# Attention score matmuls in two halves of the array's rows, four query stacks, and a quantization step split between ScalarE and GpSimd

## The chip, the cores and the metric

The kernel runs on one core of one Trainium2 chip. The metric is the device time in microseconds, the median of three runs; lower is better. TensorE's clock has two levels, 1.2 and 2.4 GHz, and the profile shows the granted share as PEclk (1.00 is 2.4 GHz).

## What is computed

The input x has shape (4, 512, 512), and everything is in float32.

```python
xn = layernorm(x)
q = (xn @ wq) as 32 heads of 16;  k = xn @ wk;  v = xn @ wv   # one k and one v for all heads
scores = q k^T / sqrt(16), causal;  probs = softmax(scores)
s = (probs @ v) @ wo
def linear8bit(x, W, b):            # columns of x with absmax > 3 go unquantized
    y = quant_rows(x_inliers) @ quant_rows(W).T + x_outliers @ W.T + b
    # quant_rows: scale = absmax/127 of the row, round(a/scale) * scale
h = linear8bit(xn, W1, b1)          # W1 is 2048 x 512
g = silu(linear8bit(h, W2, b2))     # W2 is 512 x 2048
out = x + s * g
```

## The kernel before, in words

Accuracy near float32 comes from splitting each operand into a high part in fp32r (the type that TensorE streams in one pass) and a low part, which is what the high part leaves over. A product is the sum of high x high, high x low and low x high.

There are three stages, each a block in which every engine has its own hand-written queue, joined by semaphores, with a barrier of all engines between them.

1. Preparation: layernorm, transposes, q, k and v (`a_order`, lines 163 to 174). The queries stay in `big_h` and `big_l` with features on partitions. The keys are copied several times down the partitions into `km` and `ks`: six groups of 16 rows (line 182), of which a mask in `cols` keeps the three that belong to head parity p (lines 415 to 421), so that there are two versions, p = 0 and p = 1. GpSimd builds the masks and the two step patterns `later_q` and `later_k` (lines 230 to 288), which make later keys lose inside the diagonal block of the first pass.
2. Attention, in 16 units `u` of 8 heads, one unit for each batch and 128 features. For a unit, 12 transfers (`stack_queries`, line 151) copy queries into one of three stacks: 96 rows with two heads each (high, low, high), 4 rows for the row maxima and 28 of the step pattern. The first pass (`max_piece`, lines 972 to 993) computes scores with queries on partitions, and VectorE reduces each of 24 PSUM pieces of 256, 384 or 512 columns to row maxima (line 914). These are transposed (line 1052), copied by ScalarE (line 852), and put into the stack by one transfer (line 730), so that the second pass (`scores`, line 995) gives scores with the maximum subtracted and keys on partitions. ScalarE exponentiates 22 pieces of 384 or 512 columns (line 835), GpSimd masks the diagonal blocks (line 817), and TensorE multiplies by the values in four column groups of 32 (`pv`, line 1009). VectorE transposes and inverts sums, GpSimd divides, and the unit's rows go back to `big_h` and `big_l`. `project` (line 1033) multiplies the attended rows by `wo`. Beside this runs, for one tile of 128 rows in each unit, the quantization of xn (`quantize_x`, line 698): GpSimd masks the outlier columns, VectorE takes the absmax, the scale and the reciprocal, then in one instruction multiplies xn by it and adds the magic number (line 715), GpSimd takes the magic number off (line 790), ScalarE scales back (line 845).
3. The two large products of the feed-forward part (lines 1783 to 1785 and 1806 to 1808), which the change leaves as they are but for one wait.

The order of the attention stage is one counter `g` of steps, 24 a unit (`CH`). In each step every engine does its share in program order: TensorE first one first-pass piece, then one piece of scores of a unit whose steps run `CH + LAG` = 35 later, then what tables such as `PV_AT`, `NORM_AT` and `XSCALE_AT` (lines 607 to 624) place in that step. PSUM has three banks for the first pass (`MAXB`), three for scores (`STB`), one for probs x values (`PVB`) and one for all else. A first-pass piece n waits for the reduction of piece n - 3 (line 980), a scores piece for the exponential of piece n - 3 (line 1003):

```python
if n >= NMAX:
    pe.wait_ge(s_red, n - NMAX + 1)
...
if n >= NST:
    pe.wait_ge(s_exp, n - NST + 1)
```

Outside the steady part stand the first 35 steps, in which only the first pass runs, and the drain after the last first-pass piece: the scores of the last units, 12 tile transposes for the next stage (line 1078), and projections.

## Time and profile before

| | |
|---|---|
| median of 3 runs | 802.34 us (799.99 to 802.61) |
| profiled execution, its time | 802.84 us |
| its span | 801.1 us |
| TensorE matmul busy | 764.9 us (95%) |
| VectorE busy | 638.7 us (80%) |
| ScalarE busy | 402.7 us (50%) |
| GpSimd busy | 257.6 us (32%) |

The profile is one execution. Busy times are the union of an engine's instructions, from start to end. Instructions of one engine overlap at their ends, so the work of a queue is better read from the distance between the starts of two instructions that follow each other. Matmul ends are modelled. A bracket behind a row gives the idle time before it and what ended that.

### The profile page before, as it was taken

Reading aid. Unit: us, or ns where it says so; the run is one execution under the profiler, and the core shown is the slowest. Engines: PE = TensorE matmul, PEld = TensorE weight load, DVE = VectorE, ACT = ScalarE, POOL = GpSimd, SP = SyncE. Lnnn points to the kernel's source line nnn. Section 1 sums busy time; section 2 is a strip of 40 time slices with the busy share of each in tenths; the row PEclk is TensorE's granted clock in tenths of the full one; section 3 lists DMA queues with packets and bytes.
Section 4 is the critical chain, followed back from the end, with each engine's and each line's share of the span. In section 5 each row is a group of like instructions: output and inputs, shape, how many; then the busy total and the mean of one; then the engine's idle time right before and its main releaser. Section 6 shows DMA issues by size and latency. Waiting matters only on the chain. (4 is left out here: it accounts for less than half of the span.)

```text
span 801.1 us, 12089 instructions
## 1 busy us (share of the span) xinstructions
PE 764.9 (95%) x4253; PEld 579.5 (72%) x4253; DVE 638.7 (80%) x1094; ACT 402.7 (50%) x683; POOL 257.6 (32%) x335
## 2 busy tenths in 40 slices
PE   4999999999999999999999999999997999999995
PEld 3877665556676666775578888788886788888884
DVE  7988989999999899995537476666658998599957
ACT  3454166767677676777634554544553333122212
POOL 7313135555555555554621110110100000036504
PEclk9999589999999999999999999999999999999998
DMA  7421303333322223334554444222013778536982
GB/s 258 153 106 53 86 11 91 82 80 92 90 81 83 82 81 95 89 113 123 161 192 159 143 158 144 81 78 79 27 47 97 251 220 259 164 106 219 334 287 105
DMA packets 58348, 103.37 MB, mean 129 GB/s; under 512 B 8480, under 2 KB 16688, under 8 KB 56752
## 3 DMA queue, kind: packets, MB, share of 16 engines
q1 hardware_dynamic: 58288, 102.60, 40.3%
q8 instruction: 34, 0.56, 0.3%
q14 instruction: 26, 0.21, 0.1%
HBM read 52.76 MB, written 36.70 MB: 112 GB/s over the span
## 5 line engine op out<-in xcount | busy, mean ns | idle before, releaser
L914 DVE TENSOR_REDUCE rowmax<-ps 128x2 f32<-128x512 f32 (+3 forms) x384 | 210.9, 591 | 20.7 <-PE ps L991 18.8
L835 ACT ACTIVATE probs<-ps 128x512 f32<-128x512 f32 (+1 forms) x352 | 175.2, 557 | 72.4 <-PE ps L1004 70.7
L991 PE MATMUL ps<-km,stack 128*128 128x256 f32 (+3 forms) x512 | 151.0, 350 | 2.0 <-PEq L187 1.9
L1004 PE MATMUL ps<-stack,ks 128*128 128x512 f32 (+1 forms) x352 | 133.1, 388 | 2.6 <-ACT probs L835 2.6
L991 PEld LDWEIGHTS ps<-km,stack 128*128 128x128 f32 (+1 forms) x512 | 96.0, 201 | 42.2 <-DVE rowmax L914 22.5
L817 POOL TENSOR_SCALAR_AFFINE_SELECT probs<-probs 128x512 f32<-128x512 f32 x128 | 81.0, 641 | 79.1 <-ACT probs L835 77.6
L1806 PE MATMUL ps<-big_h 128*128 128x512 f32 x256 | 100.4, 392 | 2.4 <-issue 2.0
L1808 PE MATMUL ps<-big_h,big_l 128*128 128x512 f32 x256 | 100.3, 392 | 0.0
L1807 PE MATMUL ps<-big_l,big_h 128*128 128x512 f32 x256 | 100.2, 391 | 0.0
L1017 PE MATMUL ps<-probs,vones 128*32 128x512 f32 (+3 forms) x1024 | 82.2, 439 | 0.2 <-POOL probs L817 0.2
L1004 PEld LDWEIGHTS ps<-stack,ks 128*128 128x128 f32 x352 | 67.5, 192 | 11.9 <-ACT probs L835 6.3
L1806 PEld LDWEIGHTS ps<-big_h 128*128 128x128 f32 x256 | 48.3, 189 | 12.8 <-issue 3.0
L1017 PEld LDWEIGHTS ps<-probs,vones 128*32 128x32 f32 x1024 | 26.7, 109 | 41.3 <-issue 28.2
L1808 PEld LDWEIGHTS ps<-big_h,big_l 128*128 128x128 f32 x256 | 48.3, 189 | 10.2
L1807 PEld LDWEIGHTS ps<-big_l,big_h 128*128 128x128 f32 x256 | 48.3, 189 | 10.0
L1783 PE MATMUL ps<-big_h,w_high_first 128*128 128x512 f32 x128 | 51.9, 406 | 1.6 <-PEq L689 1.6
L1438 ACT ACTIVATE h_on<-ps,b_col,w_scale 128x512 f32<-128x512 f32 x36 | 28.0, 779 | 48.8 <-PE ps L1785 48.8
L1783 PE MATMUL ps<-big_h,w_high_second 128*128 128x512 f32 x128 | 51.9, 406 | 0.6 <-DVE w_low_second L1505 0.6
L1477 ACT CAST big_h<-habs 128x1024 fp32r<-128x1024 f32 x31 | 32.4, 1045 | 39.0 <-DVE habs L1586 23.3
L1784 PE MATMUL ps<-big_l,w_high_second 128*128 128x512 f32 x128 | 50.5, 395 | 0.0
L1785 PE MATMUL ps<-big_h,w_low_second 128*128 128x512 f32 x128 | 50.5, 395 | 0.0
L1784 PE MATMUL ps<-big_l,w_high_first 128*128 128x512 f32 x128 | 50.5, 395 | 0.0
(227 smaller groups left out, 1384.3 us busy)
## 6 DMA issues: line engine op xcount, KB each, us to landing
stack<-big_h SPq DMA_DIRECT2D x128, 64.0 KB, 2.0
h_scratch<-hs SPq DMA_DIRECT2D x7, 1024.0 KB, 4.5
hload<-h_scratch SPq DMA_DIRECT2D x14, 512.0 KB, 5.4
xn_scratch<-xa SPq DMA_DIRECT2D x4, 1024.0 KB, 4.4
stack<-big_l SPq DMA_DIRECT2D x64, 64.0 KB, 2.0
xi<-xn_scratch SPq DMA_DIRECT2D x16, 256.0 KB, 2.8
xe_scratch<-xm SPq DMA_DIRECT2D x16, 256.0 KB, 2.3
w2n<-in_L_ffn_W_dram SPq DMA_DIRECT2D x4, 1024.0 KB, 6.7
```

What stands on the lines that cost most here:

```text
L817: nc.gpsimd.affine_select(out=d, in_=d, compare_op=ALU.is_ge, fill=0.0, base=0, pattern=[[0, NPAIR], [1, P]], channel_multiplier=-1).then_ ...
L835: nc.scalar.activation(probs[p][:, o:o + nh * w], ps[:, STB[n % NST], 0:nh * w], ACT.Exp).then_inc(s_exp, 1)
L914: nc.vector.tensor_reduce(dst, src, AX_X, ALU.max).then_inc(s_red, 1)
L991: last = nc.tensor.matmul(dst, stack[u % 3][rows, hp, P * qt:P * (qt + 1)], km[rows, u // KT, p0:p0 + npar, keys], start=True, stop=True)
L1004: ins = nc.tensor.matmul(ps[:, STB[n % NST], 0:nh * w].rearrange("p (h q) -> p h q", h=nh), ks[:, u // KT, p, P * kt:P * (kt + 1)], stack[ ...
L1017: ins = nc.tensor.matmul(ps[32 * j:32 * j + 32, PVB, P * kt:T], vones[:, u // KT, kt, :], probs[p][:, o:o + w], start=(kt == 0), stop=(kt ...
L1783: nc.tensor.matmul(dst, w1h[f % 2][:, k, :], big_h[:, k, t], start=(k == 0), stop=False)
L1784: nc.tensor.matmul(dst, w1h[f % 2][:, k, :], big_l[:, k, t], start=False, stop=False)
L1785: last = nc.tensor.matmul(dst, w1l[f % 2][:, k, :], big_h[:, k, t], start=False, stop=(k == KT - 1))
L1806: nc.tensor.matmul(ps[:, i, :], hqh[m % RB][:, t], w2h[m % RB], start=(kk == 0), stop=False)
L1807: nc.tensor.matmul(ps[:, i, :], hqh[m % RB][:, t], w2l[m % RB], start=False, stop=False)
L1808: return nc.tensor.matmul(ps[:, i, :], hql[m % RB][:, t], w2h[m % RB], start=False, stop=(kk == FT - 1))
```

## The change

The two head groups of a unit now lie in partitions 0 to 63 and 64 to 127: in each half 48 rows of one head's query and key parts, 2 rows for the maxima and 14 of the step pattern (two finer patterns, 10 steps of 2^12 and a factor of 32). One version of `km` and `ks` serves both. Every score matmul becomes two, one in each half of the array's rows with a PSUM bank of its own, issued one behind the other. Pieces are packed to full banks: 20 reductions and 20 exponentials a unit, all of 512 columns, in place of 24 and 22. The columns of `wq` and rows of `wo` are reordered to fit, `wo` by eight transfers; a unit's queries come by 6 transfers of 128 KB instead of 12 of 64 KB, the maxima by two transfers instead of one. There are four stacks. A unit has 20 steps. In `quantize_x` the multiply-and-add of VectorE (line 715) goes: ScalarE multiplies by the scale, GpSimd adds the magic number and then takes it off. The last combination of the row maxima becomes a reduction of three rows (128x24 to 128x8).

```diff
-        km = sa("km", [P, B, 2, T], F32R)
-        ks = sa("ks", [P, B, 2, T], F32R)
+        km = sa("km", [P, B, T], F32R)
+        ks = sa("ks", [P, B, T], F32R)
+        NSTK = 4
+        HALF_ROWS, KEPT = P // 2, 3 * HD
...
-            for hp in range(NPAIR):
-                src = slice(2 * HD * hp, 2 * HD * (hp + 1))
+            for a in range(2):
+                src = slice(HALF_ROWS * a, HALF_ROWS * (a + 1))
                 for n, part in enumerate((big_h, big_l, big_h)):
+                    lo = HALF_ROWS * a + HD * n
+                    sp.dma_start(stack[u % NSTK][lo:lo + HD, :, :].bitcast(F32),
+                                 part[src, f, tok].bitcast(F32)).then_inc(s_sq[u % NSTK], 16)
...
-                        for p in range(2):
-                            step(nc.vector.tensor_scalar(km[:, g, p, :], kvh, cols[:, p:p + 1], None,
-                                                         ALU.mult))
...
+                        step(nc.vector.tensor_scalar(ks[:, g, :], kvh, cols[:, 0:1], None, ALU.mult))
+                        ins = nc.vector.scalar_tensor_tensor(out=ks[:, g, :], in0=kvl, scalar=cols[:, 1:2],
+                                                             in1=ks[:, g, :].bitcast(F32),
+                                                             op0=ALU.mult, op1=ALU.add)
...
-        CH = 24
+        CH, NB = 20, 10
+        def pieces_of(c):
+            v, m = divmod(c // 2, 5)
+            hp = 2 * v + m // 2
+            if m == 4:
+                return [(2 * v + h, 1, own, 2 * P * h + P * own) for h in range(2) for own in (False, True)]
+            if m % 2:
+                return [(hp, 2, False, 0), (hp, 2, True, 2 * P), (hp, 0, True, 3 * P)]
+            return [(hp, 3, False, 0), (hp, 3, True, 3 * P)]
+        def scores_of(i):
+            return [[(0, 0, 1, 0)], [(0, 1, 1, 0)], [(1, 0, 1, 0), (3, 0, 1, 3 * P)],
+                    [(1, 1, 1, 0), (3, 1, 1, 3 * P)], [(2, 0, 2, 0)]][i]
...
-        GROUPS = [(0, 1), (2, 3)]
+        GROUPS = [(0, 1, 3), (2,)]
...
-        LAG = 11
+        LAG = 10
-        PV_AT = {11: (0, 0), 16: (0, 1), 22: (1, 0), 27: (1, 1)}
-        NORM_AT = {19: 0, 27: 1, 30: 2, 33: 3}
-        SHARE_AT, HIGH_AT, LOW_AT = 30, 34, 33
-        XLOAD_AT, XMASK_AT, XSCALE_AT, XROUND_AT, XBACK_AT, XSTORE_AT = -1, 15, 21, 25, 26, 30
+        PV_AT = {10: (0, 0), 14: (0, 1), 18: (1, 0), 22: (1, 1)}
+        NORM_AT = {16: 0, 24: 1, 26: 2, 29: 3}
+        SHARE_AT, HIGH_AT, LOW_AT = 25, 29, 28
+        XLOAD_AT, XMASK_AT, XSCALE_AT, XROUND_AT, XBACK_AT, XSTORE_AT = -1, 12, 16, 22, 24, 28
...
-        EVENLY = (3, 7, 12, 16)
+        EVENLY = (3, 7, 11, 13)
...
-                if part == 3:
-                    dve.wait_ge(s_xst, 3 * i + 3)
-                    nc.vector.scalar_tensor_tensor(out=xm[:, :], in0=xi[:, :], scalar=xs[:, 0:1],
-                                                   in1=magic_row[:, :], op0=ALU.mult,
-                                                   op1=ALU.add).then_inc(s_xt, 1)
...
                     u = unit_at(g, XROUND_AT)
                     if u >= 0:
                         pool.wait_ge(s_xt, u + 1)
+                        nc.gpsimd.tensor_tensor(xm[:, :], xm[:, :], magic_row[:, :],
+                                                ALU.add).then_inc(s_xg, 1)
+                        pool.wait_ge(s_xg, u + 1)
                         nc.gpsimd.tensor_tensor(xm[:, :], xm[:, :], magic_row[:, :],
                                                 ALU.subtract).then_inc(s_xr, 1)
...
+                    u = unit_at(g, XSCALE_AT + 4)
+                    if u >= 0:
+                        act.wait_ge(s_xst, 3 * u + 3)
+                        nc.scalar.activation(xm[:, :], xi[:, :], ACT.Copy, scale=xs[:, 0:1]).then_inc(s_xt, 1)
...
+                def max_pair(u, c):
                     n = CH * u + c
...
+                    if n + 1 >= NMAX:
+                        pe.wait_ge(s_red, n + 2 - NMAX)
+                    pieces = pieces_of(c)
+                    for hp, qt, own, at in pieces:
                         keys = slice(P * qt, P * qt + P) if own else slice(0, P * qt)
+                        for a in range(2):
+                            rows = slice(HALF_ROWS * a, HALF_ROWS * a + (HALF_ROWS if own else KEPT))
+                            dst = ps[:, MAXB[(n + a) % NMAX], at:at + keys.stop - keys.start]
+                            ins = nc.tensor.matmul(dst, stack[u % NSTK][rows, hp, P * qt:P * (qt + 1)],
+                                                   km[rows, u // KT, keys], start=True, stop=True)
+                            if (hp, qt, own, at) == pieces[-1]:
+                                ins.then_inc(s_max, 1)
+
+                def score_pair(u, s):
+                    p, i = divmod(s // 2, NB // 2)
                     n = 2 * NB * u + s
                     if s == 0:
+                        pe.wait_ge(s_sm[u % NSTK], 32 * (u // NSTK + 1))
+                    if n + 1 >= NST:
+                        pe.wait_ge(s_exp, n + 2 - NST)
+                    parts = scores_of(i)
+                    for kt, h, nh, at in parts:
                         w = T - P * kt
+                        for a in range(2):
+                            rows = slice(HALF_ROWS * a, HALF_ROWS * (a + 1))
+                            dst = ps[:, STB[(n + a) % NST], at:at + nh * w].rearrange("p (h q) -> p h q", h=nh)
+                            ins = nc.tensor.matmul(dst, ks[rows, u // KT, P * kt:P * (kt + 1)],
+                                                   stack[u % NSTK][rows, 2 * p + h:2 * p + h + nh, P * kt:T],
+                                                   start=True, stop=True)
+                            if kt == parts[-1][0]:
+                                ins.then_inc(s_st, 1)
...
-                        max_piece(*divmod(g, CH))
+                    if g < CH * U and g % 2 == 0:
+                        max_pair(*divmod(g, CH))
...
+                    if u >= 0 and s_ % 2 == 0:
+                        score_pair(u, s_)
```

## Rows read from the trace of the kernel before

**Rows 1.** The page's slices of the span: the rows of TensorE and its clock.

```profile
PE   4999999999999999999999999999997999999995
...
PEclk9999589999999999999999999999999999999998
```

**Rows 2.** Busy time of one stretch: length, then each engine's busy time, PEclk, DMA share, GB/s.

```profile
240.00:260.00 20.00, 20.00 (x145) 13.78 (x147) 18.45 (x40) 14.41 (x30) 11.29 (x15) 1.00 0.29 83
```

**Rows 3.** Timeline of all engines in one unit (start, us): GpSimd's subtraction, twice.

```profile
245.22 1.29 POOL L790 TENSOR_TENSOR xm<-xm,magic_row 128x512 f32<-128x512 f32 x1 [2.77 <-DVE xm L715]
...
263.51 1.29 POOL L790 TENSOR_TENSOR xm<-xm,magic_row 128x512 f32<-128x512 f32 x1 [2.77 <-DVE xm L715]
```

**Rows 4.** The same timeline: matmuls of the two passes and of the projection.

```profile
247.33 0.39 PE L1042 MATMUL ps<-woh,big_h 128*128 128x512 f32 x1
...
247.55 0.40 PE L1043 MATMUL ps<-wol,big_h 128*128 128x512 f32 x1
...
248.20 0.34 PE L1004 MATMUL ps<-stack,ks 128*128 128x384 f32 x1
...
248.37 0.28 PE L991 MATMUL ps<-km,stack 128*128 128x256 f32 x1
...
248.49 0.34 PE L1004 MATMUL ps<-stack,ks 128*128 128x384 f32 x1
```

**Rows 5.** The same timeline: probs x values in four column groups, and what follows it.

```profile
245.67 0.86 PE L1017 MATMUL ps<-probs,vones 128*32 128x256 f32 x16
...
246.45 0.50 PE L991 MATMUL ps<-km,stack 128*128 128x256 f32 x2
...
251.28 1.71 PE L1017 MATMUL ps<-probs,vones 128*32 128x512 f32 x16
...
252.92 0.45 PE L991 MATMUL ps<-km,stack 96*128 96x384 f32 x1
...
253.20 0.40 PE L1004 MATMUL ps<-stack,ks 128*128 128x512 f32 x1
```

**Rows 6.** Timeline of VectorE in the same unit: a reduction of 512 columns and its follower.

```profile
260.45 0.68 DVE L914 TENSOR_REDUCE rowmax<-ps 128x4 f32<-128x512 f32 x1
261.05 0.14 DVE L708 TENSOR_SCALAR xs<-xs 128x1 f32<-128x1 f32 x1
```

**Rows 7.** Groups by line and form in the attention stage (busy us, mean ns).

```profile
L914 DVE TENSOR_REDUCE rowmax<-ps 128x2 f32<-128x512 f32 x128 | 81.8, 680 | 0.9 <-PE ps L991 0.6
...
L914 DVE TENSOR_REDUCE rowmax<-ps 128x1 f32<-128x384 f32 x128 | 68.2, 550 | 18.1 <-PE ps L991 17.2
...
L1017 PE MATMUL ps<-probs,vones 128*32 128x512 f32 x256 | 34.1, 605 | 0.0
...
L715 DVE SCALAR_TENSOR_TENSOR xm<-xi,xs,magic_row 128x512 f32<-128x512 f32 x16 | 11.9, 745 | 0.1
```

**Rows 8.** Timeline of ScalarE in the drain: an exponential and its follower.

```profile
385.30 0.63 ACT L835 ACTIVATE probs<-ps 128x512 f32<-128x512 f32 x1
385.79 0.64 ACT L840 CAST big_h<-tb 128x512 fp32r<-128x512 f32 x1
```

**Rows 9.** The same timeline: the way of the row maxima into the stack.

```profile
257.36 0.56 ACT L852 CAST w_low_first<-ps 16x512 fp32r<-16x512 f32 x1
...
257.95 0.69 SPq L730 DMA_DIRECT2D stack<-w_low_first  x1
```

**Rows 10.** DMA issues (the page's last part): KB each, median us to landing.

```profile
stack<-big_h SPq DMA_DIRECT2D x128, 64.0 KB, 2.0
```

**Rows 11.** Timelines of TensorE and VectorE where the attention stage begins.

```profile
81.53 14.68 PE L991 MATMUL ps<-km,stack 128*128 128x256 f32 x38 [1.90 <-PEq L187]
...
100.79 0.80 PE L1004 MATMUL ps<-stack,ks 128*128 128x512 f32 x1
```

**Rows 12.** Timeline of TensorE: first tile transposes in the drain, first matmul of stage 3.

```profile
363.91 0.63 PE L1078 MATMUL ps<-ident,tail_rows 128*128 128x128 f32 x4
...
408.99 0.47 PE L1783 MATMUL ps<-big_h,w_high_first 128*128 128x512 f32 x1 [1.62 <-PEq L689]
```

245 lines of the change are left out of this document (110 added, 135 removed).

## The prediction, made before the changed kernel ran

> **What bounds the kernel now.** I first read the slices of the span [rows 1]: TensorE is busy nearly throughout, and its clock is at the upper level except in one stretch near the start of attention. Then the busy time by stretch [rows 2]: from 240 to 260 us TensorE is busy for all 20 us and VectorE for 18.45. Both are close, so the bound has to be told by adding up queues. The unit's length comes from one instruction that each unit has once: it starts at 245.22 and at 263.51 us, 18.29 us apart [rows 3].
>
> TensorE's queue in a unit, by distances between starts [rows 4]: a matmul of 512 columns takes 0.23 us, one of 384 takes 0.18 (248.20 to 248.37), one of 256 takes 0.12. The first pass is, for each of four head pairs, one of 256, four of 256 (two pieces of two matmuls), one of 512 and two of 384: 5 x 0.12 + 0.23 + 2 x 0.18 = 1.19, so 4.8 us. The scores, for each of two parities, are seven of 512 and four of 384: 2.33, so 4.7 us. Probs x values takes 1.64 us for its first group (251.28 to 252.92) and 0.78 for its second (245.67 to 246.45) [rows 5]; twice each is 4.8, and with about 0.1 of wait on each side of the four groups (the next matmul begins 0.28 us after the one at 252.92, though 384 columns take 0.18) 5.6 us. The projection is 12 x 0.23 = 2.8 and the transposes of the maxima 0.6. The sum is 18.5 us, against 18.29 measured: TensorE's queue sets the unit.
>
> VectorE's queue: a reduction of 512 columns takes 0.60 us from start to start [rows 6], though its own duration is 0.68 [rows 7]; 0.08 overlaps. 384 columns take 0.55 less 0.08, 0.47 [rows 7], so 256 take 0.34. Four times (0.34 + 3 x 0.60 + 2 x 0.47) is 12.3 us; the three transposes 1.9, reciprocals 0.4, the quantization 0.73 and 0.66 for line 715 (0.745 less 0.08 [rows 7]), the maxima's small steps 0.5: 16.5 us. That is only 1.8 us below TensorE, and it caps the gain.
>
> **TensorE after the change.** The score matmuls hold the same 10,240 columns in each pass, but in pairs, one per half of the rows. Whether halves overlap is not shown by the trace of before, since every matmul there takes all rows. The nearest row is probs x values: in 128x32 form, the 256 matmuls of 512 columns last 605 ns each and yet add up to only 34.1 us of busy time [rows 7], 0.13 us each, so the four column groups run together. I take it that two row halves do the same; bounds are fully together and fully one behind the other.
>
> Together, a pair costs what one costs. A pair with 128 columns has no row; half of the 0.12 of 256 columns is its lower bound, 0.06, and the whole 0.19 that a weight load takes its upper. I take 0.11, nearest to the 0.12 at which a matmul and the load under it repeat. The first pass has, for each two heads of a half, two windows of (384, 128), two of (256, 128, 128) and one of four times 128: 2 x 0.29 + 2 x 0.34 + 0.44 = 1.70, so 3.4 us a unit. The scores have for each parity three of 512 and two of (384, 128): 1.27, so 2.5 us. Both together: 5.9 in place of 9.5, 3.6 us less.
>
> Against this stands a switch between forms. After the column-grouped matmuls the first full one starts late and its follower 0.1 later again [rows 5]: counted as 0.3 us for a round trip: about 0.1 at the way in, 0.1 before the matmul at 252.92 and 0.1 before its follower. Now the projection (four places a unit) and the maxima's transposes also stand as full-row work between half-row pairs: 5 more round trips. Bounds are 0 and 0.4 us each; I take 0.3, the measured kind, so 1.5 us. The sum is 5.9 + 5.6 + 2.8 + 0.6 + 1.5 = 16.4 us.
>
> The row [rows 5] shows that a form change costs TensorE about 0.3 us. The Trainium skill, page "TensorEngine Tiling (Array Packing)", section "Key Properties", says that a change of tiling mode drains the engine; that speaks against this change. By the rule all five new places pay, and the sum is the 16.4 above; were it wrong for row halves, it would be 14.9.
>
> **VectorE after the change.** 20 x 0.60 = 12.0 in place of 12.3; line 715 gone, -0.66; the three-row reduction against the old maximum, within 0.05 either way (24 inputs; 0 to 0.1 us). So 12.0 + 1.9 + 0.4 + 0.7 + 0.6 = 15.6 us.
>
> **How the queues meet.** Before, TensorE waited for the reduction three pieces back; now a pair waits for the one two before its second bank, so it may start when the first reduction of the pair ahead is done, and has only the second, 0.60 us, to deliver. From the wait to data it needs about 0.1 for the weights, the starts of the parts (0.18 to 0.33) and the last one's time of 0.2 to 0.25, so 0.55 to 0.75 us, where 0.60 is covered. That is 0.05 us on most pairs and 0.15 on the (4 x 128) ones, 0.4 us a unit when nothing else hides it. Then TensorE's two heavy windows: after steps 10 and 18 it does probs x values for key blocks 0, 1 and 3 at once. The first group of before has 7 column blocks in 1.64 us, 0.1 of it switch, so 0.22 a block; 8 blocks are 1.7 us, with the switch 2.0, with the pairs 2.5 and 2.7 us, while VectorE has 1.65 (the maxima's casts) and 1.3 us of work. A lead of 0.6 us is all that VectorE's queue can have; 0.3 and 0.8 us are lost. 15.6 + 0.4 + 1.1 = 17.1 us a unit.
>
> **ScalarE and GpSimd.** ScalarE: 0.49 us a start-to-start exponential of 512 columns [rows 8], 384 about 0.1 less (estimated from its fewer columns); 14 x 0.49 + 8 x 0.39 = 10.0 before, 20 x 0.49 = 9.8 after, and the new multiply. That has no row on ScalarE with this form; the scaling back at line 845 is 0.63 from start to start (bounds 0.49 to 0.63, I take 0.63). With 2.1 us of other work it is 12.5 of 17.1 us, covered; the waits of ScalarE for TensorE are what shrinks. GpSimd gets one more pass of 1.29 us [rows 3], 10.4 to 11.7 us a unit. It sits at step 22, ahead of the mask at step 3 of the next unit and ScalarE's scaling back at step 24; the mask is needed at step 10. If it is late, TensorE's probs x values waits, and all first-pass pairs behind it; seven steps of 0.85 us against about 4 us of GpSimd work cover it. At no cost.
>
> **Transfers.** The queries move the same 768 KB in half the issues and one unit earlier: nothing. The maxima: copy at 257.36, issue at 257.95, 0.69 us [rows 9]; the second issue adds 0.69. Before, some 4 us pass until the first scores; now from step 4 to step 10 there are 5.1 us at 0.85 a step, and copy, two issues and 2 us of landing [rows 10] are 3.9. Covered, with 1 us to spare; behind this wait stands all of TensorE.
>
> **Outside the steady part.** Preparation: VectorE has two more small low parts ahead of the first transposed rows, +0.3 us; the key steps saved and GpSimd's changed constants lie beside TensorE's work; wo's eight issues come while SyncE has nothing due. The first steps: 35 steps lasted from 81.53 to some 101.6 us [rows 11], 20.1 us, at the lower clock [rows 1]. Now 30 steps, 15 pairs of 1.2 us; at the lower level columns take twice as long, so about 0.25 us a pair is not covered: 15 x 1.45 = 21.8, +1.7 us. The drain lasts from 363.9 to 409.0 us [rows 12]; its 30 steps of scores in place of 35 spare TensorE 3 us, and its transposes between them add up to 12 round trips of which part is paid already: -1.5 us (-3 to +2).
>
> **The sum.** From the start of the scores (101.6) to the drain (363.9) the old kernel passes 349 steps, 0.752 us each, so 18.05 us for 24. That is 14.5 units: 14.5 x (18.05 - 17.1) = 13.8 us less. With +0.3, +1.7 and -1.5, the change is -13.3 us on the profiled execution's 802.84, so 789.5; that execution lies 0.5 above the median of 802.34, so the forecast is **789 us**.
>
> **Rivals.** (B) Row halves change place without a drain, and the lead is enough: VectorE sets the unit at 15.6 + 0.6 = 16.2. For it: between halves and full rows the columns' grouping stays the same. Against it: the form change that is shown does cost. 14.5 x 1.85 = 26.8 less, 776 us. (C) Halves don't overlap: the pairs cost 11.9 instead of 5.9 us, TensorE 22.4 us a unit, +4.3 x 14.5 = +62, about 864 us. Against it stand the overlapping column groups. It decides from the point at which a pair costs 1.3 times one matmul (5.9 x 1.3 = +1.8 us). (D) Half-row pairs overlap but their weight loads don't hide: 128 columns cost 0.19 and a round trip 0.4. There are 20 slots of 128 columns a unit, +1.6, and +0.5 for the switches: TensorE has 18.5 us, and with what the heavy windows lose 18.7: +0.65 x 14.5 = +9, 811 us. It needs both near their upper bounds, and is slower from 18.1 a unit on. (E) TensorE's clock stays at the lower level, which it had while only the first pass ran [rows 1], since it has idle time again: the queue of 16.4 us would be some 30, over 950 us. Against it: it rose once scores ran beside the first pass, and at the lower level TensorE would have no idle time.
>
> The Trainium skill, page "TensorE: Matmul & The Clock Gate", section "The mechanism" of its part on packing, says that loads and matmuls of different row groups overlap. By it C is wrong and A or B holds; no run here shows it yet.
>
> **How the numbers follow.** Chances: forecast (A) 0.52, B 0.18, C 0.10, D 0.17, E 0.03. A, B and D, with D's less complete forms, lie between 772 and 810. A difference under 0.3% (2.4 us) is no more than a measurement of this kernel can tell. A and B are faster; a third of D is within it or just faster. Faster 0.74, same 0.05, slower 0.21.
>
> **What would show it.** Two score matmuls a few ns apart, and a pair no longer than one (A, B, D); 17.1 us between two subtractions of line 790; VectorE busy over 90% with waits for the first pass after steps 10 and 18; a start about 0.3 us late after each projection; ScalarE's waits shorter; the lower clock still there in the first steps. The prediction is wrong if a pair takes two matmuls' time, if GpSimd's masks or the maxima's transfer hold TensorE, or if clock levels change within the steady part.

## The result, and the profile of the changed kernel

The changed kernel takes 809.89 us in the median of 4 runs (808.69 to 813.15), the kernel before 802.05 (799.99 to 802.61, 4 runs). The ratio is 1.0109, with a 95% interval of 1.0073 to 1.0145. The forecast was 789 us, range 772 to 810. The change made the kernel slower by 1.1% and not faster by 1.7%: the sign was wrong, though the time lies 0.1 us inside the stated range, whose slow end lies next to rival D. The profiled execution took 810.79 us, its span is 808.9 us, 7.8 us more than that of before.

The first view is the page's slices of the span, which answer to [rows 1].

```profile
PE   3999578888999999999889999999997999999995
...
PEclk9999658999999999999999999999999999999998
```

TensorE, which had nines from the second slice to the 30th, now has 5, 7 and eights behind the start of attention, and the low clock there lasts longer. The view of busy time by stretch makes this exact. Its columns are the stretch and its length, then busy us of TensorE, its weight loads, VectorE, ScalarE, GpSimd, the granted clock, the DMA share and GB/s. First the kernel before:

```profile
80.00:100.00 20.00, 18.47 (x51) 12.84 (x51) 18.34 (x37) 2.12 (x3) 3.79 (x2) 0.55 0.36 86
...
140.00:160.00 20.00, 19.38 (x135) 12.03 (x134) 19.33 (x43) 14.54 (x32) 11.71 (x17) 1.00 0.30 81
160.00:180.00 20.00, 19.36 (x143) 11.16 (x142) 18.84 (x41) 13.78 (x28) 11.30 (x15) 1.00 0.31 81
```

Then the same view of the changed kernel, with the stretch of [rows 2] as its last row:

```profile
80.00:100.00 20.00, 10.92 (x67) 7.96 (x66) 14.78 (x24) 0.66 (x2) 5.68 (x3) 0.67 0.62 87
100.00:120.00 20.00, 14.91 (x88) 10.08 (x92) 16.12 (x28) 8.29 (x14) 3.35 (x5) 0.50 0.32 48
120.00:140.00 20.00, 17.18 (x164) 8.77 (x160) 17.06 (x34) 13.00 (x25) 10.55 (x15) 0.84 0.35 68
140.00:160.00 20.00, 16.82 (x172) 9.27 (x164) 15.95 (x32) 12.93 (x24) 11.92 (x15) 0.88 0.38 68
160.00:180.00 20.00, 17.15 (x160) 9.20 (x158) 16.56 (x33) 13.47 (x26) 11.51 (x15) 0.83 0.34 69
180.00:200.00 20.00, 16.82 (x176) 9.42 (x178) 17.59 (x34) 14.46 (x29) 11.84 (x15) 0.91 0.38 69
...
240.00:260.00 20.00, 19.41 (x191) 11.08 (x190) 18.08 (x35) 15.29 (x30) 12.90 (x17) 1.00 0.56 110
```

From 120 to 200 us the clock was 1.00 throughout before, with TensorE busy 18.8 to 20.0 us in 20; now it alternates between its two levels (2.4 and 1.2 GHz), with means of 0.83 to 0.91, and TensorE is busy 17 us in 20. In this part of the stage there is no projection yet (it begins at step 127), so TensorE has the least to do here, and the change took more from it. Only from 200 us on does the forecast's unit exist. There GpSimd's subtraction, the mark of [rows 3], shows its length in the timeline:

```profile
240.33 1.28 POOL L823 TENSOR_TENSOR xm<-xm,magic_row 128x512 f32<-128x512 f32 x1
...
257.75 1.28 POOL L823 TENSOR_TENSOR xm<-xm,magic_row 128x512 f32<-128x512 f32 x1
```

That is 17.42 us, against 18.29 before and 17.1 forecast. Inside it the timeline of TensorE (answering to [rows 4, 5]) is one queue with a single gap:

```profile
246.54 0.50 PE L1021 MATMUL ps<-km,stack 48*128 48x384 f32 x4 [0.59 <-DVE rowmax L948]
246.85 0.47 PE L1039 MATMUL ps<-stack,ks 64*128 64x512 f32 x2
247.25 1.93 PE L1053 MATMUL ps<-probs,vones 128*32 128x512 f32 x24
249.11 0.56 PE L1021 MATMUL ps<-km,stack 48*128 48x256 f32 x6
249.51 0.45 PE L1039 MATMUL ps<-stack,ks 64*128 64x512 f32 x2
...
256.50 0.45 PE L1039 MATMUL ps<-stack,ks 64*128 64x512 f32 x2
256.88 0.50 PE L1078 MATMUL ps<-woh,big_h 128*128 128x512 f32 x1
257.22 0.40 PE L1079 MATMUL ps<-wol,big_h 128*128 128x512 f32 x1
257.45 0.40 PE L1080 MATMUL ps<-woh,big_l 128*128 128x512 f32 x1
257.78 0.56 PE L1021 MATMUL ps<-km,stack 48*128 48x256 f32 x6
...
263.96 0.44 PE L1021 MATMUL ps<-km,stack 48*128 48x384 f32 x2 [0.59 <-DVE rowmax L948]
```

The two halves of a pair overlap: two matmuls of 512 columns (256.50) last 0.45 us together, where one lasts 0.39 to 0.40 (257.22). A switch of form shows as well: line 1078 keeps the queue 0.34 us and line 1080 0.33, line 1079 between them 0.23. Adding up the distances from 246.54 to the gap before 263.96 gives 16.8 us of queue and 0.59 of wait for a reduction. VectorE is busy 15.9 us of the 17.42.

Where the 7.8 us of span come from, read from the first matmul of each stage, from the row where a unit's maxima are cast (line 1001, line 966 before), and from the first matmul of the FFN:

| part | before, us | after, us | difference | forecast |
|---|---|---|---|---|
| preparation, to the first attention matmul | 81.5 | 84.4 | +2.9 | +0.3 |
| from there to the first unit's maxima | 13.8 | 17.7 | +3.9 | +1.7 |
| unit 1 | 15.8 | 17.1 | +1.2 | |
| units 2 to 6 | 88.4 | 94.3 | +5.9 | |
| the last nine units | 164.5 | 156.2 | -8.3 | |
| units 1 to 15 together | 268.8 | 267.7 | -1.1 | -13.8 |
| from the last maxima to the FFN | 44.9 | 47.0 | +2.1 | -1.5 |
| FFN | 392.1 | 392.2 | +0.1 | 0 |

The forecast cut its terms at the first matmul of the scores and not at the first maxima. From the first matmul of the stage to there it is 25.3 us now (84.41 to 109.74) against 19.3 before (81.53 to 100.79, which the forecast took as 20.1), so by its own bounds its +1.7 measured +5 to +6; the part behind the first maxima lies in unit 1 of the table.

Units 2 to 6 took 17.6, 17.5, 17.5, 17.5 and 18.3 us before and take 18.5, 19.3, 18.3, 19.3 and 19.0 now. The groups by line of the page say the same in sum. VectorE's reductions of 512 columns take 682 ns each, as before (680 in [rows 7]), but now wait 33 us for the first pass (19 before), and the first pass waits 30 us for them (before, its matmuls stood idle 2.0 us in all):

```profile
L948 DVE TENSOR_REDUCE rowmax<-ps 128x4 f32<-128x512 f32 (+2 forms) x320 | 208.5, 682 | 34.7 <-PE ps L1021 32.9
...
L1021 PE MATMUL ps<-km,stack 64*128 64x128 f32 (+3 forms) x896 | 98.1, 324 | 31.5 <-DVE rowmax L948 29.6
```

### The profile page after: what moved, and what is told of

It reads as the page before. It is cut to its first block and busy times, and to the rows that moved or that the text cites. A ratio compares the mean times of both kernels' runs of the same rounds, so it can differ in the third digit from the quotient of the medians.

```text
span 808.9 us, 12809 instructions
## 1 busy us (share of the span) xinstructions
PE 742.6 (92%) x4733; PEld 538.5 (67%) x4733; DVE 623.9 (77%) x1008; ACT 413.7 (51%) x669; POOL 274.5 (34%) x338
## 3 DMA queue, kind: packets, MB, share of 16 engines
q1 hardware_dynamic: 56864, 102.60, 44.9%
## 5 line engine op out<-in xcount | busy, mean ns | idle before, releaser
L948 DVE TENSOR_REDUCE rowmax<-ps 128x4 f32<-128x512 f32 (+2 forms) x320 | 208.5, 682 | 34.7 <-PE ps L1021 32.9
L871 ACT ACTIVATE probs<-ps 128x512 f32<-128x512 f32 x320 | 176.4, 595 | 69.5 <-PE ps L1039 69.4
L1021 PE MATMUL ps<-km,stack 64*128 64x128 f32 (+3 forms) x896 | 98.1, 324 | 31.5 <-DVE rowmax L948 29.6
L1021 PEld LDWEIGHTS ps<-km,stack 64*128 64x128 f32 (+1 forms) x896 | 69.9, 205 | 81.0 <-DVE rowmax L948 61.2
L1053 PE MATMUL ps<-probs,vones 128*32 128x512 f32 (+3 forms) x1024 | 88.6, 467 | 0.0
L1039 PE MATMUL ps<-stack,ks 64*128 64x512 f32 (+2 forms) x448 | 76.4, 382 | 2.1 <-ACT probs L871 2.0
L1821 PE MATMUL ps<-big_h,w_low_first 128*128 128x512 f32 x128 | 51.2, 400 | 0.0
```

What stands on the lines that cost most here:

```text
L871: nc.scalar.activation(probs[p][:, o:o + T], ps[:, STB[n % NST], :], ACT.Exp).then_inc(s_exp, 1)
L948: nc.vector.tensor_reduce(dst, src, AX_X, ALU.max).then_inc(s_red, 1)
L1021: ins = nc.tensor.matmul(dst, stack[u % NSTK][rows, hp, P * qt:P * (qt + 1)], km[rows, u // KT, keys], start=True, stop=True)
L1039: ins = nc.tensor.matmul(dst, ks[rows, u // KT, P * kt:P * (kt + 1)], stack[u % NSTK][rows, 2 * p + h:2 * p + h + nh, P * kt:T], start=Tru ...
L1053: ins = nc.tensor.matmul(ps[32 * j:32 * j + 32, PVB, P * kt:T], vones[:, u // KT, kt, :], probs[p][:, o:o + w], start=(kt == 0), stop=(kt ...
L1821: last = nc.tensor.matmul(dst, w1l[f % 2][:, k, :], big_h[:, k, t], start=False, stop=(k == KT - 1))
```

## The experiments

Unless a run says otherwise, its edit is made in the changed kernel and its ratio is to the kernel before. "Units" are the distances between the casts of the maxima. The stretches of low clock are those of the trace's granted clock. The kernel before was measured again beside each group of runs and gave medians of 800.9 to 802.1 us, so times from different groups can be compared to about 1 us only. The times of e1 to e5, e8, e10, e11, e14 and e15 lie outside both ranges that had been expected for them; what is read from these runs rests on their units, waits and clock.

### Does the quantization, moved to ScalarE and GpSimd, matter?

Run e3 puts the multiply and add back on VectorE, and takes out ScalarE's multiply and GpSimd's addition.

```
+                    nc.vector.scalar_tensor_tensor(out=xm[:, :], in0=xi[:, :], scalar=xs[:, 0:1],
+                                                   in1=magic_row[:, :], op0=ALU.mult,
+                                                   op1=ALU.add).then_inc(s_xt, 1)
...
-                                                ALU.add).then_inc(s_xg, 1)
-                        pool.wait_ge(s_xg, u + 1)
-                        nc.gpsimd.tensor_tensor(xm[:, :], xm[:, :], magic_row[:, :],
...
-                        act.wait_ge(s_xst, 3 * u + 3)
-                        nc.scalar.activation(xm[:, :], xi[:, :], ACT.Copy, scale=xs[:, 0:1]).then_inc(s_xt, 1)
```

> The changed kernel with the multiply-and-add of xn back on VectorE, and neither ScalarE's multiply nor GpSimd's addition. If VectorE's queue sets the unit at the full clock, each of the 9 units of 17.4 us grows by 0.5 to 0.7 us, the low-clock ones by 0 to 0.7: 814 to 818 us. If TensorE's heavy windows or ScalarE set the unit, ScalarE loses 0.6 us of work and the time stays within 1 us of 809.9.

Measured: 812.67 us, ratio 1.0147 (1.0119 to 1.0176). The full-clock units stay at 17.4 us with 0.7 us more work on VectorE in each; only the alternating ones grow (19.1, 19.4, 20.1, 20.0, 19.0, together 3.3 us). TensorE's timeline has the same gap of 0.59 us in the same place:

```profile
248.93 0.51 PE L1019 MATMUL ps<-km,stack 48*128 48x384 f32 x4 [0.59 <-DVE rowmax L946]
```

VectorE's busy time in a unit goes from 15.9 to 16.5 us of 17.42, and the new instruction fills a wait of 0.56 us that VectorE has at this place in the changed kernel (256.13 to 256.69). So at full clock VectorE's queue as a whole does not set the unit, as the forecast had it. TensorE's queue does, and with it one wait for a reduction.

Run e4 makes only this part of the change, in the kernel before: ScalarE multiplies one step behind the reciprocal, GpSimd adds.

```
+                    u = unit_at(g, XSCALE_AT + 3)
+                    if u >= 0:
+                        act.wait_ge(s_xst, 3 * u + 3)
+                        nc.scalar.activation(xm[:, :], xi[:, :], ACT.Copy, scale=xs[:, 0:1]).then_inc(s_xt, 1)
```

> The kernel before, with only that step moved: ScalarE multiplies (one step later than VectorE's reciprocal), GpSimd adds and subtracts the magic number. TensorE's queue sets the unit there at 18.3 us, so that 0.66 us off VectorE give nothing: within 1 us of the kernel before. If VectorE's 16.5 us shared the bound with TensorE, up to 0.3 us a unit would come off: 797 to 798 us.

Measured: 814.55 us, 1.0164 (1.0131 to 1.0196), units of 19.6 us instead of 18.3. The timeline of ScalarE shows why:

```profile
250.05 0.72 ACT L826 ACTIVATE xm<-xi,xs 128x512 f32<-128x512 f32 x1 [2.32 <-DVE xs L713]
250.68 1.55 ACT L838 ACTIVATE probs<-ps 128x512 f32<-128x512 f32 x3
253.56 0.72 ACT L848 ACTIVATE xm<-xm,xs 128x512 f32<-128x512 f32 x1 [1.33 <-POOL xm L789]
```

ScalarE stands 2.32 us before the multiply until VectorE has the scale (line 713), and 1.33 us before the scaling back; the exponentials are queued behind both. Run e8 makes the same edit with later steps.

```
-        XLOAD_AT, XMASK_AT, XSCALE_AT, XROUND_AT, XBACK_AT, XSTORE_AT = -1, 15, 21, 25, 26, 30
+        XLOAD_AT, XMASK_AT, XSCALE_AT, XROUND_AT, XBACK_AT, XSTORE_AT = 3, 15, 21, 28, 32, 34
...
-                    u = unit_at(g, XSCALE_AT + 3)
+                    u = unit_at(g, XSCALE_AT + 5)
```

> The kernel before with the split quantization step as in the run before it with that edit, but with ScalarE's multiply two steps later than there (step 26, five behind the absmax), GpSimd's two passes at 28, the scaling back at 32 and the store at 34. There ScalarE stood 2.3 us in each unit for VectorE's reciprocal, the unit took 19.6 us and the kernel 814.6. If that wait was the whole loss, the unit returns to 18.3 us and the kernel to 801 to 803 us; if GpSimd's second pass or ScalarE's work costs in itself, it stays above 806.

Measured: 803.58 us, 1.0027 (1.0014 to 1.0039), units of 17.5 and then 18.6 us. The wait for the scale is gone and the one before the scaling back is 0.47 us. So 11 of the 13 us that e4 lost stood in these two waits; the edit moves the load, the rounding, the scaling back and the store as well, and doesn't tell the two apart. The split itself gains nothing before the row halves are there. In the changed kernel, taking it back (e3) costs 2.8 us in the medians, with intervals of the ratio that overlap, and it costs them in the units in which the clock alternates.

### The first 30 steps: lead or clock?

While only the first pass runs, TensorE and VectorE wait for each other in turn. The timeline of TensorE, then that of VectorE, in the changed kernel:

```profile
84.41 0.50 PE L1021 MATMUL ps<-km,stack 48*128 48x384 f32 x4 [1.89 <-PEq L200]
85.67 0.56 PE L1021 MATMUL ps<-km,stack 48*128 48x256 f32 x6 [0.75 <-DVE rowmax L948]
...
90.27 1.12 PE L1021 MATMUL ps<-km,stack 48*128 48x128 f32 x8 [0.78 <-DVE rowmax L948]
92.16 0.80 PE L1021 MATMUL ps<-km,stack 48*128 48x384 f32 x4 [0.78 <-DVE rowmax L948]
...
84.92 2.63 DVE L948 TENSOR_REDUCE rowmax<-ps 128x1 f32<-128x512 f32 x4 [0.99 <-PE ps L1021]
...
89.52 1.29 DVE L948 TENSOR_REDUCE rowmax<-ps 128x4 f32<-128x512 f32 x2 [0.39 <-PE ps L1021]
91.42 1.29 DVE L948 TENSOR_REDUCE rowmax<-ps 128x2 f32<-128x512 f32 x2 [0.61 <-PE ps L1021]
```

Both banks of a pair become complete only with its last two matmuls, at the low clock. A pair takes 1.57 to 1.90 us, where the two reductions need 1.29. The first two pairs still ran at the upper level: the second starts 1.26 us after the first, and VectorE has four reductions without a gap (84.92). So the wait takes both, the pair and the lower level. Run e5 puts the parts of one half ahead of those of the other, each with a wait of its own, in these 30 steps.

```
-                    for hp, qt, own, at in pieces:
...
-                        for a in range(2):
...
+                    apart = n < CH + LAG
...
+                    order = ([(q, a) for a in range(2) for q in pieces] if apart
+                             else [(q, a) for q in pieces for a in range(2)])
+                    for (hp, qt, own, at), a in order:
+                        if apart and n + a >= NMAX and (hp, qt, own, at) == pieces[0]:
+                            pe.wait_ge(s_red, n + a + 1 - NMAX)
```

> The changed kernel, but in the first 30 steps (15 pairs) the first-pass matmuls of the first half go ahead as soon as their own bank is free (the reduction three pieces back) and those of the second half follow behind the later wait: the halves run one after the other, no work is added. If the 0.3 to 0.6 us that VectorE waits at each pair come from the lead of one reduction (pair theory), the wait goes and the first steps shrink from 25.3 to about 20 us: 804 to 806 us. If they come from the lower clock alone, columns that now run twice as long one by one at that clock leave VectorE waiting as before or longer: 809 to 814 us.

Measured: 807.09 us, 1.0079 (1.0044 to 1.0114). The stretch from the first matmul to the first maxima is 13.5 us instead of 17.7, about what the kernel before needs, and TensorE's timeline has one group without a gap there:

```profile
89.55 4.87 PE L1025 MATMUL ps<-km,stack 48*128 48x128 f32 x20
```

The 3.9 us are explained by the pairs at this level. Unit 1 then takes 18.1 us instead of 17.1, so that 2.8 us of the 4.2 are left in the kernel's time, and the alternation behind it stays (18.6, 19.3, 18.3, 19.3, 19.0).

Run e1 asks it of the clock instead: two rounds of added matmuls, one on each half of the rows, in each of these steps. Their result is read by nothing.

```
+                        if g < CH + LAG:
+                            for _r in range(2):
+                                for a in range(2):
+                                    rows = slice(HALF_ROWS * a, HALF_ROWS * (a + 1))
+                                    nc.tensor.matmul(ps[:, (PVB, STB[2])[a], :], woh[rows, 0, 0:P],
+                                                     woh[rows, 1, :], start=True, stop=True)
```

> The changed kernel; behind each of the 15 first-pass pairs of the first 30 steps TensorE also multiplies two rounds of 512 columns in both halves, into banks not yet in use; nothing reads them. In the changed kernel these steps last 25.3 us, at the lower clock, with VectorE waiting 0.29 to 0.61 us for each pair. Theory 1 (clock): TensorE is too idle for the upper clock; kept busy it gets it back within some us, a pair delivers in time, the 25.3 us become 20 to 21.5, and the kernel takes 805 to 807 us. Theory 2 (pairs): the wait is the fixed way from a finished reduction to the next pair of banks, and more work can only delay it: 809 to 814 us.

Measured: 808.36 us, 1.009 (1.0061 to 1.012). The low stretch falls from 34.1 us to two of 10.2, and the first maxima come 16.6 us after the start, 1.0 less. Unit 1 takes 15.3 us instead of 17.1; units 2 to 6 alternate as before, up to 20.0 us, and are 1.5 us longer together. Added work here moved the clock and bought 1.5 us in the medians, which is hardly more than the groups of runs differ by.

### Units 2 to 6: is it the clock?

Run e6 spreads the halves as in e5, up to step 126. TensorE is busy for longer without having more work.

```
-                    apart = n < CH + LAG
+                    apart = n < 127
```

> The same for all first-pass pairs up to step 127, the stretch without projections. It adds 3.4 us of TensorE time to units in which TensorE has that much idle, so it also makes it busier. Theory clock: the units of 18.2 to 19.3 us come down to 17.4 or below, 797 to 801 us together with the first steps. Theory that busy TensorE delays VectorE in the lockstep: units stay at 18 to 19 us, 804 to 808 us.

Measured: 806.24 us, 1.0061 (1.0042 to 1.008), units of 17.8, 20.0, 18.2, 19.4, 18.2 and 20.1. Two rows by stretch:

```profile
140.00:160.00 20.00, 19.10 (x165) 11.72 (x161) 16.32 (x33) 13.55 (x26) 11.11 (x14) 0.83 0.39 68
160.00:180.00 20.00, 19.02 (x170) 11.16 (x168) 17.52 (x35) 14.63 (x29) 11.80 (x16) 0.91 0.40 71
```

TensorE is busy 19 us in 20 and the clock falls all the same. Busy time that comes from stretching the same matmuls does not hold it.

Run e10 adds work instead: three matmuls of 512 columns over all rows, at four places in every 20 steps, from step 31 on.

```
+                    if CH + LAG <= g < CH + LAG + CH * (KT - 1) + T0 + 3 and (g - CH - LAG) % CH in (1, 5, 7, 17):
+                        pe.wait_ge(s_mh, (g - MAX_AT - 1) // CH)
+                        for k in range(3):
+                            nc.tensor.matmul(ps[:, MISCB, :], woh[:, k, 0:P], woh[:, k, :], start=True, stop=True)
```

> The changed kernel with three full-row matmuls of 512 columns at steps 1, 5, 7 and 17 of each unit between steps 30 and 127, and nothing added in the first 30 steps. Clock theory: from the first upper-clock stretch on, the clock stays up and the units of 18.3 to 19.3 us take 17.4: 802 to 804 us. If the added work only delays: 810 to 815 us.

Measured: 808.33 us, 1.0087 (1.0068 to 1.0105). All units from the third on take 17.4 us and the clock doesn't fall again before 415.8 us; the first two, entered at the low clock (up to 125.6 us), take 20.8 and 19.4: there an added group lasts 1.65 us, at full clock 0.97. The clock was the cause of units 3 to 6, and what it gave back was spent in front of it.

Run e2 is e1 and e10 together:

> As the run before, and besides three full-row matmuls of 512 columns at steps 1, 5, 7 and 17 of each unit from step 30 to step 127, where the changed kernel has no projection yet; nothing reads them. In the changed kernel those units last 18.2 to 19.3 us and the clock goes up and down; later ones, with real projections in these places, last 17.4. Theory 1 (clock): the early units come to 17.4 to 17.6 us although TensorE does 3 us more in each; with the first steps' gain the kernel takes 797 to 801 us. Theory 2: the early units are long for another reason than the clock (the lockstep of pairs), the added work lengthens or leaves them: 808 to 815 us.

Measured: 803.66 us in the median of 10 runs, which spread from 796.69 to 808.16; 1.0017 (0.998 to 1.0055). The three fastest (796.7, 796.7 and 798.8 us) had the highest mean clock, 0.989 to 0.990; among the others time and clock don't go together (799.4 at 0.977, 808.2 at 0.982). The trace is of one of the longer runs: the first maxima come after 17.7 us, as without e1's part, and the clock is low for 41.0 us. Why the runs differ is not known. Run e12 is e5 and e10 together:

> The changed kernel with the halves one behind the other in the first 30 steps (-3 us by the run of that) and the full-row additions up to step 127 (-7 us by the clock theory): 798 to 801 us, so level with the kernel before or 0.3% under it. If the two gains hide each other: 803 us or more.

Measured: 803.86 us, 1.004 (1.0028 to 1.0052): first maxima after 13.5 us as in e5, units of 22.8 and 20.0, then 17.4. Run e11 is e10 with the added matmuls on rows 0-63 alone:

```
-                            nc.tensor.matmul(ps[:, MISCB, :], woh[:, k, 0:P], woh[:, k, :], start=True, stop=True)
+                            nc.tensor.matmul(ps[:, MISCB, :], woh[0:HALF_ROWS, k, 0:P], woh[0:HALF_ROWS, k, :], start=True, stop=True)
```

> The same with each added matmul in rows 0 to 63 alone, the same columns and times, so that TensorE is busy as long. If the time that TensorE is busy holds the clock, it is like the run with full rows: 802 to 804 us. If half-row matmuls count less, as the run with the halves apart up to step 127 suggests (TensorE busy 19 of 20 us and the clock still falling), the units stay at 18 to 19.5 us: 808 to 812 us.

Measured: 805.44 us, 1.0056 (1.0041 to 1.0071): 19.3, 19.2, 16.7, 18.2, 16.7 and then 17.4, one low stretch at 155.1 us. A unit with added half-row work takes 16.7 us, 0.7 less than with the same columns on all rows. The form doesn't change on the way in and out: in e13, which has the same groups, a score pair and the group behind it keep the queue for 0.95 us (161.84 to 162.79), in e10 for 1.28 (129.30 to 130.58).

If added work pays only once the clock is up, it should stand only there. Run e13 has e5's edit, and e11's added matmuls from step 51 on; e14 has two of the four groups, e15 six. The condition of e13, in place of e11's:

```
-                    if CH + LAG <= g < CH + LAG + CH * (KT - 1) + T0 + 3 and (g - CH - LAG) % CH in (1, 5, 7, 17):
+                    if 2 * CH + LAG <= g < CH + LAG + CH * (KT - 1) + T0 + 3 and (g - CH - LAG) % CH in (1, 5, 7, 17):
```

> Two edits of the changed kernel together. In the first 30 steps the pieces of one half all stand ahead of those of the other, as in the run that did that alone (807.09 us, its last event at 802.8). In steps 50 to 126, which is after TensorE's clock has come back to 2.4 GHz and not before, four groups of three added 512-column matmuls on array rows 0-63 stand in every 20 steps, whose result nothing reads. Theory that the clock falls because of idle time of TensorE in the second to sixth unit, and that added matmuls cost only while the clock is low: the units that begin after 140 us take 16.7 to 17.4 us instead of 17.4 to 20, no low stretch lies between 140 and 400 us, and the time is 798 to 802. Theory that the clock of these units is decided by how they were entered, whatever is added later: low stretches remain and the time is 805 to 809, or more, since the added matmuls are then paid at the low clock.

The condition of e14, in place of e13's:

```
-                    if 2 * CH + LAG <= g < CH + LAG + CH * (KT - 1) + T0 + 3 and (g - CH - LAG) % CH in (1, 5, 7, 17):
+                    if 2 * CH + LAG <= g < CH + LAG + CH * (KT - 1) + T0 + 3 and (g - CH - LAG) % CH in (5, 17):
```

> The same with two groups of three added matmuls in every 20 steps instead of four, from step 50 to 126. If the amount of TensorE work decides: between the run without added work (807) and the one with four groups, with some low stretches left, 801 to 805. If half the work is enough to hold the clock: no low stretch between 140 and 400 us and 797 to 801.

The condition of e15, in place of e13's:

```
-                    if 2 * CH + LAG <= g < CH + LAG + CH * (KT - 1) + T0 + 3 and (g - CH - LAG) % CH in (1, 5, 7, 17):
+                    if 2 * CH + LAG <= g < CH + LAG + CH * (KT - 1) + T0 + 3 and (g - CH - LAG) % CH in (1, 5, 7, 11, 15, 17):
```

> The run with late fillers again, with six groups of three added matmuls in every 20 steps instead of four, in steps 50 to 126 as there. It had 800.2 us, with two low stretches of TensorE's clock left (134.4 and 185.6 us, 3.4 us each) and units of 18.3 and 19.0 us at them, and units of 16.7 between. Theory that the clock follows the work that TensorE has: both stretches go, the six added groups leave the units at 16.9 to 17.4, and the time is 797 to 800, a little under the kernel before. Rival: four groups were all that fits in the idle time (19.05 us busy of 20), so that two more cost .7 us each in every unit and nothing is gained by the clock: 801 to 804.

Busy time by stretch, 160 to 180 us, of e13, e14 and e15 in this order:

```profile
160.00:180.00 20.00, 19.05 (x205) 11.60 (x197) 18.92 (x38) 15.45 (x29) 13.79 (x18) 1.00 0.40 74
```

```profile
160.00:180.00 20.00, 18.18 (x167) 10.46 (x165) 16.52 (x34) 13.66 (x27) 11.18 (x14) 0.83 0.40 70
```

```profile
160.00:180.00 20.00, 18.49 (x169) 10.73 (x168) 15.85 (x31) 13.06 (x24) 11.17 (x14) 0.91 0.34 70
```

e13: 800.23 us, ratio 0.9988 (0.9974 to 1.0002). The units are 18.0, 19.9, 18.3, 16.7, 16.7, 19.0 and then 17.4; of the low stretches behind the first there are two left, at 134.4 and 185.6 us; none had been expected behind 140. e14: 807.18 us, 1.0081 (1.0062 to 1.01), as e5 without any added work. e15: 813.85 us, 1.0153 (1.0137 to 1.0168), units of 20.3, 20.4, 20.4 and 21.1 us, with a low stretch in each. Four groups hold the clock for two units and, with e5's edit, give back the whole loss; two do nothing; six are too many. In e15 the clock theory in its simple form, more work and therefore no low stretch, missed. The rival's price was too small too: it gave 0.7 us for an added group, and the unit grew by 3.7 for two. A low stretch costs its unit about 1.6 us (18.3 against 16.7 in e13), so about 2 us are the two groups and 1.6 the clock. Which of these two came first isn't settled.

### The preparation

Timeline of ScalarE, casting wq's high part into its new order, first in the kernel before and then in the changed one:

```profile
11.52 0.61 ACT L318 CAST wqh<-w1t_first 128x512 fp32r<-128x512 f32 x1
...
13.29 2.05 ACT L310 CAST xth<-ps 128x512 fp32r<-128x512 f32 x4 [0.64 <-PE ps L478]
```

```profile
11.37 1.17 ACT L333 CAST wqh<-w1t_first 128x512 fp32r<-128x512 f32 x1
12.32 1.15 ACT L333 CAST wqh<-magic_row 128x512 fp32r<-128x512 f32 x1
```

The copy in the new order writes neighbouring elements 16 bytes apart. It takes 1.15 us for 128x512 instead of 0.61, and on VectorE (line 396) 1.18 instead of 0.69. The first k/v matmul starts at 17.38 us instead of 15.23. By then TensorE has stood still for 3.73 us (1.43 before), and its matmuls of 512 columns follow each other at 0.43 us, the lower level, up to 22.0 us, where they did at 0.23 before. So the first q matmul starts at 22.36 us instead of 18.04. Run e7 lets VectorE make the low part after the k/v rows.

```
-                for k in range(KT):
-                    weight_low(by_head(wql[:, k, :]), in_features(wq_in[k]), by_head(wqh[:, k, :]), 5 + k)
...
+                            if g == 0:
+                                for kk in range(KT):
+                                    weight_low(by_head(wql[:, kk, :]), in_features(wq_in[kk]),
+                                               by_head(wqh[:, kk, :]), 5 + kk)
```

> The changed kernel; the four low parts of wq on VectorE (1.1 to 1.2 us each since they write and read every fourth element, 0.6 before) stand behind the low parts of the first transposed rows instead of ahead of them. In the changed kernel TensorE's first k and v matmul starts at 17.4 us, 2.2 later than before, and the clock falls meanwhile. If VectorE's queue is what delays it, it starts near 14.5 and attention begins near 82 instead of 84.4: 806.5 to 808 us. If the rest of preparation has slack anyway the time stays at 809.9.

Measured: 810.08 us, 1.011 (1.0072 to 1.0149). k/v starts at 15.30, but its matmuls run at the lower level and the q matmuls then wait from 19.35 to 21.30 us for the low part. Attention begins at 84.1 us: the wait has moved. Run e9 writes in order and reads every 32nd element:

```
-            return row.rearrange("p (f h x) -> p f h x", f=KT, h=NPAIR)
+            return row.rearrange("p (f h x) -> p f x h", f=KT, h=NPAIR)
...
-            return row.rearrange("p (f x h) -> p f h x", f=KT, h=NPAIR)
+            return row.rearrange("p (f x h) -> p f x h", f=KT, h=NPAIR)
```

> The changed kernel with the copies of wq walked in the other order: they write one element after the other and read every 32nd, instead of reading one after the other and writing every fourth. In the changed kernel one copy takes ScalarE 1.15 us and its low part VectorE 1.18 us, 0.6 and 0.7 before. If it is the writes at a distance that cost, both fall back to 0.6 to 0.7, k and v start at 15.4 us and attention 2 to 3 us earlier: 807 us. If any distance costs, they stay near 1.1 and the time at 809 to 811 us.

Measured: 807.97 us, 1.0103 (1.0072 to 1.0133). The casts on ScalarE still take 1.12 to 1.13 us, the low parts on VectorE 1.03 to 1.05, and attention begins at 83.6. The distance costs on either side of the copy. Whether e7 or e9 gave anything back is not shown: in the eleven other runs with the changed preparation attention begins at 83.4 to 85.2 us, against 81.5 to 82.3 in the three with the old one. That the strided copies make up the whole +2.9 is read from the timelines; no run has the new layout without them.

## Why the prediction was wrong, step by step

**What was right.** The halves overlap, so C fell, and the clock did not stay down for good, so E fell. The unit at full clock was forecast at 17.1 us and takes 17.4. Of its terms VectorE's 15.6 us hold: it is busy 15.9 us in a unit. TensorE's 16.4 are 16.8: the first-pass pairs take 0.33, 0.40 and 0.50 us where 0.29, 0.34 and 0.44 stood, and a switch of form costs a little over the 0.3 us that it had: a group of three projection matmuls keeps the queue for 0.90 us where three times 0.23 are 0.69, and the score pair ahead of it for 0.38 where its columns need 0.23, so 0.36 together. Yet the reason for 17.1 was wrong: VectorE's queue plus handshake (0.4) plus heavy windows (1.1). The queue that is packed is TensorE's, 16.8 us and the one wait of 0.59, and e3 shows that 0.7 us more on VectorE changes nothing there. VectorE's waits in a unit do add up to the forecast's 1.5 us (17.42 less 15.90, most of it in three places of 0.39 to 0.56), but they are what TensorE's queue leaves over: e3 fills one of them and the unit stays, and where TensorE has less to do at full clock (e11, e13) the unit is 16.7. The Trainium skill, page "TensorEngine Tiling (Array Packing)", section "Key Properties", says that a change of tiling mode drains the engine; these rows agree in that each change costs time. Transfers and GpSimd did not hold TensorE, as forecast, although a unit's queries landed in a median of 4.8 us and not in the 2.0 of before.

**The failed step: 14.5 units at one length.** The sum took 349 steps of before at their mean of 0.752 us and the new unit at full clock for all of them. Nine units of fifteen were of that kind, and brought -8.3 us. The first six lack the projection (it begins in the sixth), and two things were missed about them. Before, the first five took 15.8 to 17.6 us, so 17.1 would have been at most 0.5 us shorter each, and 1.7 us for all six together. And after the change TensorE has 3 us of idle time in 20, under which the clock alternates; the list of what would make the prediction wrong had named changing levels in the steady part, but in the sum they had neither a price nor a chance. Together these units are +7.2 us, and all fifteen -1.1 instead of -13.8. e10, e2 and e13 show the mechanism (17.4 or 16.7 us where the clock stays up). With 17.4 us for units 2 to 6 the changed kernel would take 7.3 us less, about 802.6, no faster than before.

**The first steps.** The term was 15 pairs with 0.25 us uncovered, 21.8 us and so +1.7; they took 25.3, and the first ten alone are +3.9. The mechanism was right and e5 confirms it (4.2 us back up to the first maxima); the size was off, since at the lower level the two banks of a pair come so late that 0.28 to 0.61 us of each pair is uncovered.

**Preparation.** It had +0.3 us for VectorE's small low parts and overlooked that the new order of wq makes every copy of it strided, and that TensorE, kept waiting, would begin at the lower level: +2.9, of which the copies' whole share is not shown by a run. A duration in a row holds for its access pattern too.

**Drain.** It had -1.5 us with +2 as the bad end; measured +2.1. TensorE's busy time there is 41.0 us against 40.3, and the other 1.3 us are waits. The spared score columns did not count, it seems, since transposes and projections, both full-row work, stand between single pairs, and each pair pays a switch on both sides. The timeline of TensorE in the drain:

```profile
387.11 0.51 PE L1039 MATMUL ps<-stack,ks 64*128 64x384 f32 x4
387.55 0.50 PE L1078 MATMUL ps<-woh,big_h 128*128 128x512 f32 x1
387.89 0.39 PE L1079 MATMUL ps<-wol,big_h 128*128 128x512 f32 x1
388.12 0.40 PE L1080 MATMUL ps<-woh,big_l 128*128 128x512 f32 x1
388.45 0.66 PE L1114 MATMUL ps<-ident,tail_rows 128*128 128x128 f32 x4
389.04 0.50 PE L1039 MATMUL ps<-stack,ks 64*128 64x512 f32 x2
...
392.01 0.66 PE L1114 MATMUL ps<-ident,tail_rows 128*128 128x128 f32 x4 [1.57 <-DMA tail_rows<-xe_scratch]
```

The pair at 389.04 keeps the queue for 0.43 us where one of its two matmuls has 0.23 us of columns [rows 4]. At 392.01 TensorE also waits 1.57 us for a tile's transfer, as it did 0.98 before, and the first matmul of the next stage waits 2.3 us instead of 1.6. No experiment was made on the drain, so this split is read from the trace and the cause is not shown.

**Rivals.** D came to nearly the measured time (811 against 809.9) by another way: weight loads were not the cause, a full-clock unit took 17.4 us and not 18.7. Its price was also low by its own count: it has 20 slots of 128 columns, and the scores add four. The reading that every matmul of before takes all rows isn't quite so, [rows 5] has one of 96; no rival rests on the difference. That the measured time came out inside the range, at D's end, is luck.

**What stays open.** What TensorE has to do for the clock to stay up. Work on all rows, added, held it (e10), and work on half of them for all but one or two stretches (e11, e13); the same work stretched did not (e6); half the addition did not (e14), and more of it did not either (e15). A kernel with the new layout that beats the one before was not found: the best, e13 with 0.9988, can't be told from it.

## What to carry to other kernels

A change that spares the bounding engine work is worth its price only in the stretches where that engine has a full queue afterwards too. List the stretches by what runs in them, take each one's length before and the second-longest queue in it, and sum over them instead of multiplying one unit. And if TensorE is left with idle time in a stretch, price the same stretch once more at the lower clock before believing the gain.

## What the runs showed of the hardware beyond that

The granted clock can fall again in mid-stage: TensorE busy 16.8 to 17.2 us in 20 went with a mean clock of 0.83 to 0.91. A busy share of 19 in 20 went with 0.83 (e6) and with 1.00 (e13), so the share alone doesn't tell which it will be. Copies that write 4-byte elements 16 bytes apart take 1.15 us on ScalarE and 1.18 on VectorE for 128x512, against 0.61 and 0.69 in order; reading every 32nd element and writing in order took 1.12 and 1.03 (e9). Two waits at the head of ScalarE's queue, 2.32 and 1.33 us in a unit, for values that VectorE and GpSimd had not finished, went with 11 us of a whole kernel (e4 against e8).
